# Perceiver layer on one core: the feed-forward block's quantisation rewritten, and its third weight prepared inside the self-attention

## The reference, cut to what matters

```python
def act_qdq(x):
    scale = jnp.maximum(jnp.max(jnp.abs(x)) / qmax, 1e-12)     # qmax = 2**15 - 1
    return jnp.clip(jnp.round(x / scale), -qmax - 1.0, qmax) * scale
def lpbq_dequant(w):                                           # 4 bits, blocks of 32
    wb = w.reshape(O, I // BLOCK, BLOCK)
    s = jnp.maximum(jnp.max(jnp.abs(wb), axis=-1, keepdims=True) / qmax, 1e-12)
    return (jnp.clip(jnp.round(wb / s), -qmax - 1.0, qmax) * s).reshape(O, I)
x = act_qdq(x)
up = act_qdq(x @ lpbq_dequant(w_up).T)
gate = act_qdq(x @ lpbq_dequant(w_gate).T)
sig = fixed_qdq_u16(jax.nn.sigmoid(gate))
gate = act_qdq(gate * sig)
o = act_qdq(gate * up)
return o @ lpbq_dequant(w_down).T
```

## Time and profile before

| | before |
|---|---|
| median of 3 runs (lowest to highest) | 1400.45 us (1395.76 to 1401.65) |
| profiled execution | 1400.91 us, of it 1398.7 us span from first to last instruction |
| TensorE, VectorE, ScalarE, GpSimd busy | 1257.7, 879.3, 723.3, 411.8 us |
| cross-attention, to the self-attention's first instruction | 1104.8 us |
| self-attention | 1104.8 to 1303.1 us |
| feed-forward block | 1303.1 us to the end |

### The profile page before, as it was taken

How to read it: one execution, slowest core, us unless ns; L and a number is a source line. 1 busy time by engine, 2 the same in 40 slices (tenths; PEclk the granted TensorE clock), 3 DMA queues, 4 the chain that set the end, 5 groups by cost and what they waited for, 6 DMA issues and landing times. The chain is left out here.

```text
span 1398.7 us, 21065 instructions
## 1 busy us (share of the span) xinstructions
PE 1257.7 (90%) x8379; PEld 939.1 (67%) x8379; DVE 879.3 (63%) x1042; ACT 723.3 (52%) x1304; POOL 411.8 (29%) x372
## 2 busy tenths in 40 slices
PE   3999999999999999899999999999999697969533
PEld 2786877777786868587868687777778443636312
DVE  5647676766766676547676767676776456513576
ACT  3655556565656556546565655655565231523152
POOL 3605051433425150414342505152342102211010
PEclk9999999999999999999999999999999798979776
DMA  4303020302021133210311203030202354250000
GB/s 154 76 1 74 7 80 1 80 1 80 18 63 50 28 78 93 74 36 2 79 42 39 60 22 79 1 80 1 76 3 63 129 95 55 35 57 1 23 0 15
DMA packets 42528, 68.19 MB, mean 49 GB/s; under 512 B 5040, under 2 KB 31152, under 8 KB 42432
## 3 DMA queue, kind: packets, MB, share of 16 engines
q1 hardware_dynamic: 40896, 66.21, 19.3%
q10 hardware_dynamic: 1536, 0.66, 0.4%
HBM read 25.89 MB, written 0.52 MB: 19 GB/s over the span
## 5 line engine op out<-in xcount | busy, mean ns | idle before, releaser
L455 DVE TENSOR_REDUCE step_max<-score_banks 128x2 f32<-128x1024 f32 x256 | 300.5, 1221 | 122.2 <-PE score_banks L579 122.2
L476 DVE TENSOR_TENSOR prob_sum<-prob_sum,probs 128x1024 f32<-128x1024 f32 x224 | 279.4, 1288 | 139.5 <-ACT probs L406 138.8
L338 POOL TENSOR_TENSOR k_split<-probs,k_split 64x512 fp32r<-64x512 f32 x128 | 163.6, 1278 | 327.6 <-ACT probs L389 323.7
L406 ACT ACTIVATE probs<-score_banks 128x1024 f32<-128x1024 f32 x181 | 181.9, 1028 | 149.4 <-PE out_ps L605 85.3
L593 PE MATMUL score_banks<-q_twice,k_split 128*128 128x256 f32 x724 | 182.2, 288 | 0.2 <-ACT probs L406 0.2
L594 PE MATMUL score_banks<-q_low_max,k_ones 128*128 128x256 f32 x724 | 178.1, 283 | 0.0
L340 POOL TENSOR_TENSOR k_split<-probs,k_split 64x512 fp32r<-64x512 f32 x128 | 163.9, 1281 | 9.6
L593 PEld LDWEIGHTS score_banks<-q_twice,k_split 128*128 128x128 f32 x724 | 138.3, 191 | 11.9 <-issue 6.2
L594 PEld LDWEIGHTS score_banks<-q_low_max,k_ones 128*128 128x128 f32 x724 | 138.5, 191 | 0.0
L331 POOL TENSOR_TENSOR w_lo<-w_raw,w_hi 128x768 fp32r<-128x768 f32 x16 | 36.2, 2260 | 336.5 <-ACT w_hi L357 336.5
L381 ACT ACTIVATE k_split<-key_banks 64x512 fp32r<-64x512 f32 x128 | 75.5, 590 | 104.7 <-PE key_banks L542 104.1
(11 more groups left out here) (207 smaller groups left out, 2169.2 us busy)
## 6 DMA issues: line engine op xcount, KB each, us to landing
k_ones<-k_split SPq DMA_DIRECT2D x128, 256.0 KB, 4.0
ctx_rows<-in_ctx_dram SPq DMA_DIRECT2D x10, 512.0 KB, 3.8
grouped_far<-dots_far SPq DMA_DIRECT2D x32, 136.0 KB
w_raw<-in_L_xattn_w_v_dram SPq DMA_DIRECT2D x14, 256.0 KB, 3.5
probs<-in_ctx_dram SPq DMA_DIRECT2D x6, 512.0 KB, 5.9
w_raw<-in_L_xattn_w_q_dram SPq DMA_DIRECT2D x16, 128.0 KB, 3.5
w_raw<-in_L_xattn_w_k_dram SPq DMA_DIRECT2D x16, 128.0 KB, 3.8
wo_pair<-in_L_xattn_w_o_dram SPq DMA_DIRECT2D x16, 128.0 KB, 2.1
```

Source lines behind the costliest of these rows:

```text
L338: pool.tensor_tensor(k_split[DH:P, A, keys], keys_staged[j % 2][0:DH], k_split[0:DH, A, keys].bitcast(F32), ALU.subtract).then_inc(k_low[A ...
L406: act.activation(probs[:, j % 2, h, :], scores_of, ACT.Exp, scale=SCALE).then_inc(exp_done, 1)
L455: dve.tensor_reduce(step_max[:, qt, :, j], score_banks[:, 2 * qt:2 * qt + 2, :], X, ALU.max).then_inc(max_done, 1)
L476: dve.tensor_tensor(prob_sum[:, h, :], prob_sum[:, h, :], probs[:, j % 2, h, :], ALU.add).then_inc(sum_done, 1)
```

## The change

In `gated_ffn` VectorE now takes each maximum itself, with the absolute value inside the reduction, straight from the PSUM banks where the operand lies there; the copies of magnitudes go. Rounding has two passes (times inverse plus constant; minus constant, times scale) without caps, since a value divided by a scale made of the largest magnitude stays within them. Passes go by chunks of 512 columns and are spread: first passes on ScalarE, second ones on VectorE for the input, the gates and the product, on GpSimd for the sigmoid, for `up` and for the gated values. Gate chunks stay in their banks until rounded. The input is rounded after its transposition. ScalarE's sigmoid table is loaded at the block's start by an activation of one column.

`w_down` moves into the second loop of `self_attention`: loaded into the gate weight's place once that is transposed, quantised by VectorE in steps 18 to 23, transposed in steps 25, 27 and 29, copied by ScalarE a step later. The last value rows of the second batch (`v_last_b1`) now lie in `qT`, so their transfer waits for the last far scores (`far_made`).

```diff
+        QUANTISE_AT = SA_STEPS + 1
+        DOWN_AT = QUANTISE_AT + W_PARTS + 1
...
+            sp.wait_ge(hidden_made, 2 * WT_BANKS)
+            load_ffn_weight(sp, down_w, w_down, down_in)
+            sp.wait_ge(far_made, PAIRS)
             sp.dma_start(v_last_b1, v_last[MEM:2 * MEM, :]).then_inc(last_in, 16)
...
+                m = down_at(n - 1)
+                if m is not None:
+                    act.wait_ge(down_made, m + 1)
+                    copy(downT[:, 2 * m:2 * m + 2, :].rearrange("p c d -> p (c d)"), bank[0]).then_inc(down_copied, 1)
...
+                if QUANTISE_AT <= n < QUANTISE_AT + W_PARTS:
+                    if n == QUANTISE_AT:
+                        dve.wait_ge(down_in, 16)
+                        dve.wait_ge(hidden_chain, 2 * W_OPS)
+                    quantise_weight(dve, n - QUANTISE_AT, down_w, w_scales, down_chain, 0)
...
+                if down_at(n) is not None:
+                    transpose_down(down_at(n))
...
-            load_ffn_weight(sp, w_down_sb[:, :], w_down, w_in)
...
-                if n == UPS:
-                    pool.wait_ge(hidden_copied, 2 * FC)
-                    pool.wait_ge(scaled, 2 * UPS + 2)
-                    round_pass(pool, UPS, 0, up[:, :, :].rearrange("p c n -> p (c n)")).then_inc(up_chain, 1)
-                    pool.wait_ge(up_chain, 1)
+            largest(INPUT)
+            largest(GATES)
+            for c in range(FC):
+                pool.wait_ge(sig_scaled, c + 1)
+                pool.tensor_scalar(sig[:, c, :], sig[:, c, :], ROUND, U_STEPS - 1.0, ALU.subtract, ALU.min
+                                   ).then_inc(sig_whole, 1)
+            largest(UPS)
+            largest(GATED)
+            for c in range(FC):
+                pool.wait_ge(up_first, c + 1)
+                pool.tensor_scalar(up[:, c, :], up[:, c, :], ROUND, scale_of(UPS), ALU.subtract, ALU.mult
+                                   ).then_inc(up_rounded, 1)
+                if c > 0:
+                    pool.wait_ge(gated_first, c)
+                    pool.tensor_scalar(sig[:, c, :], sig[:, c, :], ROUND, scale_of(GATED), ALU.subtract, ALU.mult
+                                       ).then_inc(gated_rounded, 1)
+            largest(PRODUCT)
...
+            for c in range(DC):
+                act.wait_ge(xT_made, c + 1)
+                first_pass(INPUT, xqT[:, c, :], bank[6 + c][:, :], x_first)
+            act.wait_ge(scaled, scale_ready(GATES))
+            for c in range(FC):
+                first_pass(GATES, gate[:, c, :], bank[c][:, :], gate_first)
+            for c in range(FC):
+                act.wait_ge(gate_rounded, c + 1)
+                act.activation(sig[:, c, :], gate[:, c, :], ACT.Sigmoid).then_inc(sig_made, 1)
+                act.wait_ge(sig_made, c + 1)
+                act.activation(sig[:, c, :], sig[:, c, :], ACT.Identity, bias=round_bias[:, 0:1], scale=U_STEPS
+                               ).then_inc(sig_scaled, 1)
+                copy_up(c)
...
+            def largest(which, c, src):
+                dve.tensor_reduce(limits[:, which, c:c + 1], src, X, ALU.max, apply_absolute_value=True
+                                  ).then_inc(top_read, 1)
...
+            def second_pass(which, t, done):
+                dve.tensor_scalar(t, t, ROUND, scale_of(which), ALU.subtract, ALU.mult).then_inc(done, 1)
...
+            for c in range(FC):
+                dve.wait_ge(sig_whole, c + 1)
+                dve.scalar_tensor_tensor(sig[:, c, :], sig[:, c, :], 1.0 / U_STEPS, gate[:, c, :], ALU.mult, ALU.mult
+                                         ).then_inc(gated, 1)
+                if c > 0:
+                    dve.wait_ge(gated, c)
+                    largest(GATED, c - 1, sig[:, c - 1, :])
+                largest_up(c)
...
+            for c in range(FC):
+                if c > 0:
+                    dve.wait_ge(gated_rounded, c)
+                dve.wait_ge(up_rounded, c + 1)
+                dve.tensor_tensor(sig[:, c, :], sig[:, c, :], up[:, c, :], ALU.mult).then_inc(product, 1)
+                if c > 0:
+                    dve.wait_ge(product, c)
+                    largest(PRODUCT, c - 1, sig[:, c - 1, :])
```

More of the change, by code:

```diff
@@ L1264, in project, with transpose_down @@
                 last.then_inc(proj_made, 1)
+            def transpose_down(m):
+                pe.wait_ge(down_chain, W_OPS)
+                if m == 0:
+                    pe.wait_ge(out_copied, PAIRS)
+                wait_past(pe, down_copied, m)
+                for k in range(4):
+                    last = transpose_weight(pe, down_w, DC, m * 4 + k, bank[0][:, k * P:(k + 1) * P], ident)
+                last.then_inc(down_made, 1)
             def pair_dots(b, pair, t, out):
@@ L1464, in gated_ffn, with inverse_of, scale_of, scale_ready @@
         INPUT, GATES, UPS, GATED, PRODUCT = range(5)
[L1465 to L1505, removed]
+        def inverse_of(which):
+            return limits[:, which, INV:INV + 1]
+        def scale_of(which):
+            return limits[:, which, SCL:SCL + 1]
+        def scale_ready(which):
+            return 2 * which + 2
+        def up_bank(c):
+            return bank[(FC + c) % len(bank)]
+        def of_tokens(t):
+            return sig[:, :, t * P:(t + 1) * P]
         block = stack.enter_context(nc.Block())
@@ L1532, in _ @@
+            largest(PRODUCT)
         @block.scalar
         def _(act):
[L1534 to L1541, removed]
-            xflat = xn[:, :, :].rearrange("p t d -> p (t d)")
-            for c in range(CHUNKS[INPUT]):
-                magnitudes(INPUT, c, xflat[:, c * 512:(c + 1) * 512])
@@ L1562, in _, with first_pass @@
[L1562 to L1575 removed]
+            def first_pass(which, out, src, done):
+                act.activation(out, src, ACT.Identity, bias=round_bias[:, 0:1], scale=inverse_of(which)
+                               ).then_inc(done, 1)
@@ L1586, in find_scale, with top @@
+            def top(which, read):
+                dve.wait_ge(top_read, read)
+                dve.tensor_reduce(limits[:, which, TOP:TOP + 1], limits[:, which, 0:FC], X, ALU.max).then_inc(top_found, 1)
             def find_scale(which):
                 a = limits[:, which, :]
-                dve.wait_ge(magnitude_read, BEFORE[which + 1])
-                dve.tensor_reduce(a[:, TOP:TOP + 1], a[:, 0:CHUNKS[which]], X, ALU.max).then_inc(top_found, 1)
                 dve.wait_ge(peak, which + 1)
@@ L1615, in _, with largest_up @@
+            def largest_up(c):
+                dve.wait_ge(up_copied, c + 1)
+                largest(UPS, c, up[:, c, :])
             normalise_rows(dve, x_res, xn, stats, moments, norm_chain, inverse_std)
[L1616 to L1617 removed]
             dve.wait_ge(norm_chain, NORMALISED)
+            dve.tensor_reduce(limits[:, INPUT, TOP:TOP + 1], xn[:, :, :].rearrange("p t d -> p (t d)"), X, ALU.max,
+                              apply_absolute_value=True).then_inc(top_found, 1)
@@ new lines, in _ @@
+            dve.wait_ge(gated, FC)
+            largest(GATED, FC - 1, sig[:, FC - 1, :])
+            top(UPS, 3 * FC)
+            top(GATED, 3 * FC)
+            find_scale(UPS)
+            find_scale(GATED)
+            dve.wait_ge(scaled, scale_ready(GATED))
+            dve.tensor_scalar(sig[:, 0, :], sig[:, 0, :], inverse_of(GATED), ROUND, ALU.mult, ALU.add).then_inc(gated, 1)
+            dve.wait_ge(gated, FC + 1)
+            second_pass(GATED, sig[:, 0, :], gated)
+            dve.wait_ge(gated, FC + 2)
@@ new lines, in _ @@
+            for c in range(FC):
+                if c > 0:
[5 more added lines that the diff above has]
+                    largest(PRODUCT, c - 1, sig[:, c - 1, :])
+            dve.wait_ge(product, FC)
+            largest(PRODUCT, FC - 1, sig[:, FC - 1, :])
+            top(PRODUCT, 4 * FC)
@@ L1665, in _ @@
+            find_scale(PRODUCT)
+            dve.wait_ge(scaled, scale_ready(PRODUCT))
+            t = of_tokens(0)
+            dve.tensor_scalar(t, t, inverse_of(PRODUCT), ROUND, ALU.mult, ALU.add).then_inc(product, 1)
+            dve.wait_ge(product, FC + 1)
+            second_pass(PRODUCT, t, product_rounded)
+            for t in range(1, TOK_TILES):
+                dve.wait_ge(product_first, t)
+                second_pass(PRODUCT, of_tokens(t), product_rounded)
             for t in range(TOK_TILES):
```

211 lines of the change are left out of this document (71 added, 140 removed).

## The result

The changed kernel took 1411.21 us (median of 4 runs, 1409.7 to 1412.87), the kernel before 1401.05 (4 runs) beside it: a ratio of 1.008, interval 1.0062 to 1.0098. It is slower by 0.6 to 1.0%, and 17.7 us above the forecast of 1393.5.

A forecast was written before the change was run, and what follows sets the result against it. One dependent chain over all engines, none busy throughout, was taken to bound the feed-forward block. Self-attention +2.4 and block -9.3 gave -6.9 us: 1394.0 profiled, 1393.5 at the median; range 1388.5 to 1400.

The forecast's parts named there:

- the price of GpSimd's instruction: Sigmoid and product stages: a 512-column GpSimd pass was taken at 0.68 us, scaled from 2.81 for 3072 columns.
- Rival (d): GpSimd's passes cost 1.28 like its two-operand ones: block 1.2 us slower, kernel 1404; chance 0.10 together with rival (c).
- Sigmoid stage: From the gates' scale to the gated values' scale: 20.5 us predicted, 34.52 before, a cumulative gain of 18.6 there.
- product stage: From the gated values' scale to the product's scale: 22.9 to 23.7 us predicted, against 13.22 before.
- the gates' scale: Feed-forward block: ready at 1329.2 instead of 1333.79, gain 4.5; 26.0 us from the statistics, against 30.63 before.
- rival (c): All-reduce's second and third loads slower than 5.60 us; at 11.57 each, the kernel takes 1406; chance 0.10 together with Rival (d).
- Rival (b): All five GpSimd loads at 6.77, or absolute maxima at twice 0.68 on VectorE: 1396 to 1400 us; chance 0.21.
- rival (a): Product stage: the port does not hold GpSimd up, which ends at 1364.3; block gains 11.6, kernel 1390.3; chance 0.24.
- my 11.0 us for the eleven passes: Product stage: GpSimd's second passes from 1356.0 to 1367.0, with 0.6 added for each of five VectorE multiplications.
- +2.4: Self-attention: cost in us of taking in the third weight, mainly transposes plus a transfer ahead of the far scores.
- 2.1 was taken: Self-attention: 12 more TensorE transposes in three steps after 1259 cost 2.1 us, between 1.3 and 3.4.
- The 0.3 taken for the transfer: Self-attention: 64 KB in SP's queue ahead of the far scores costs 0.3 us, between 0 and 1.1.

The follow-up runs named there:

- run 3: run 2 with the minimum moved from GpSimd's sigmoid passes into VectorE's product: 1394.53 us, ratio 0.9959 to the kernel before.
- run 2: Changed kernel with GpSimd's subtractions of a constant written as additions of the negative constant: 1400.19 us, ratio 0.9996 to the kernel before.
- run 6: Self-attention of the changed kernel with the feed-forward block of before, less the third weight's load, quantisation and transposes: 1398.85 us, ratio 0.9996.
- runs 1 and 7: Kernel before plus two different series of GpSimd passes on a tensor of their own behind its last all-reduce, to price operations; no total time given.

## Why the prediction was wrong, point by point

**The step that failed** is the price of GpSimd's instruction: "Its 512-column instruction has no row: 2.81 for 3072 columns, less 2560 at 0.83 ns (the two memsets, 3.51 and 2.02 for 4096 and 2304), is 0.68." That row is a multiply-add, and the memsets have no arithmetic; the changed kernel's passes are subtract-minimum and subtract-multiply. Measured alone they take 1.92 to 2.02, in place 1.97 to 2.42, the longest where a product of VectorE's starts beside them. The width was scaled rightly (the multiply-add at 512 columns takes 0.62 to 0.68), the operation was not asked about. Rival (d) had the right place and sign, but took its 1.28 from two-operand rows as the dear end; the true price lay outside my bounds. Its sum is off too: 0.6 more for each of the eleven passes and for the sigmoid's last one is about 7 us, which gives 1401, not 1404.

**What it cost.** Sigmoid stage: 28.62 against 21.93 in run 3, 6.7 us; product stage: 35.28 against 23.41, 11.9. Together 18.6 of the block's miss of 21.4. The rest is small: 1.4 by which run 3's sigmoid stage too is over the 20.5 of the prediction, of it 1.2 up to the end of GpSimd's last sigmoid pass, most of that ScalarE's (its six first passes take 4.13, where 3.5 was taken), and 0.3 in the load back; the gates' scale 1.2 late, 0.4 of it in the input, and most of the rest goes with a lower clock (in the changed kernel's trace the gates' matmuls ran at a granted clock of 0.78 from 1314 to 1329, in run 2's at 0.88 from 1316 to 1329, and in run 3 the stage takes 25.56). All the gaps for loads are 0.2 to 0.7 over what was taken.

**Stages that came within 1.4 us of what was worked out:** the input, the gates, the last matmuls, and with the price mended the two others. The loads were right, and rival (c) wrong: the second and third load of the all-reduce take the same 6.0 as the first's 5.8. The Trainium skill ("GPSIMD Engine Reference", section "2.1 Instruction dispatch") gives about 6 us for the first call to freshly loaded code; the gaps ahead of the all-reduces agree, and those ahead of the arithmetic, 7.1 and 7.4, are longer. Rival (b)'s dear absolute maximum does not exist (0.68), and its dearer loads are there only in part.

**The shared port:** between rival (a), no holding up, and my 11.0 us for the eleven passes. In run 3 they took 9.96 (1359.60 to 1369.56): a pass that met a multiplication of VectorE's took 1.22, one that met only a maximum 0.69. The Trainium skill ("SBUF — State Buffer", section "SBUF: two separate sides") has a VectorE instruction with two SBUF inputs and one of GpSimd's that reads SBUF exclude each other for the whole instruction, the first to start holding the port pair. That one of the two waits agrees, the rest does not: in run 3 GpSimd's pass starts 0.05 us ahead, at 1362.05, and is the one that is longer, by 0.53, while VectorE's multiplication takes its 0.69; in the changed kernel VectorE starts 0.04 behind a pass of 1.99 and is late by only 0.49 (1.18 against 0.69), not by the whole of it. The Trainium skill ("SBUF — State Buffer", section "Who interferes with whom") has a reduction never contend on this chip, and the maximum agrees: 0.68 beside GpSimd's passes at 1341.95.

**The self-attention:** +2.4 was forecast; +0.95 stands in the two traces, and run 6 finds nothing for the move as a whole. From the far scores' mixing to the block's statistics it is 43.91 us before (1259.25 to 1303.16), 45.14 after (1257.44 to 1302.58) and 44.42 in run 6 (1256.02 to 1300.44). Over all nine traces it is 43.3 to 43.9 in the three with the old code (before, runs 1 and 7) and 44.1 to 45.5 in the six with the new: 1.3 more on average for the transposes, where 2.1 was taken.

The wait for the far scores did cover the quantisation, but its fall from 11.10 to 3.89 is not all the quantisation's. That put the products off by 1.5 us (3.56 of waiting against 2.06) in each of the six new traces, and their waits for the far scores are 3.89 to 9.27, where the old ones are 10.73 to 11.67. What varies is also the speed of the first batch's products: a group of eight took 1.60 us or 0.90, the slow price for five of the eight groups before, for all eight after and for three in run 6, at granted clocks of 0.64, 0.51 (the lower level, 1.2 GHz) and 0.74 in these stretches. The 0.3 taken for the transfer in front of the far sends is not seen at the mixing, which starts 154.1 us into the self-attention after and 154.4 before.

The whole self-attention took 195.4 to 198.3 us in the three traces of the old code and 196.2 to 199.6 in the six of the new, on average 197.1 and 197.7. It varies by more than the change, and a finer number is not settled.

## What to carry to other kernels

A price is that of an engine, a width and the operations: before work goes to another engine, look for a row with the same pair of operations, and where there is none, bound it by rows with other operations too, or measure it alone behind the kernel's last use of that engine. GpSimd, which must load its program to change its kind of work, cost 5.5 to 7.7 us each way in these traces; VectorE did the same passes in 0.42 to 0.49 us each, and had been waiting for 8.1 and 19.3 us of the two stages for GpSimd's. When a stage's chain turns over to a slower helper, the wait that ends last names it at once: the chain of waits of one run pointed to the right lines.

## What the runs showed of the hardware that was not expected

GpSimd's arithmetic with constants has two prices at 3072 columns, 0.9 and 3.5 ns a column. At 512 columns there are three. Quick are multiply-add, add-multiply, multiply-multiply and the copy (0.61 to 0.70 us). One operation alone costs 1.5, so that a single addition or multiplication is dearer than either pair of both (0.7), and adding two tensors (1.26) is cheaper than adding one constant. All other pairs tried, add-add too, cost 1.92 to 2.02. Why is not shown.
